# The second of sixteen feed-forward steps in plain instead of block-product form

## What is computed

```
gate  = x @ Wg.T ;  up = x @ Wu.T               # 1600 x 4096 each
gelu  = tanh(0.797885*(gate + 0.044715*gate**3)) * gate*0.5 + gate*0.5
inter = gelu * up
out   = x1 + inter @ Wd.T                        # 1600 x 512
```

## Time and profile before

| what | us |
|---|---|
| median of three runs (lowest, highest) | 2029.73 (2028.54, 2032.24) |
| the profiled execution: its time | 2030.02 |
| the profiled execution: its span, first to last instruction | 2028.2 |
| TensorE busy | 1965.3 (97%) |
| mean granted clock of TensorE | 0.990 |

### The profile page before, as it was taken

How to read it: one execution, slowest core, us unless ns; L and a number is a source line. 1 busy time by engine, 2 the same in 40 slices (tenths; PEclk the granted TensorE clock), 3 DMA queues, 4 the chain that set the end, 5 groups by cost and what they waited for, 6 DMA issues and landing times.

```text
span 2028.2 us, 34290 instructions
## 1 busy us (share of the span) xinstructions
PE 1965.3 (97%) x11480; PEld 1891.6 (93%) x11480; DVE 1603.5 (79%) x3046; ACT 1008.6 (50%) x2344; POOL 1166.8 (58%) x1323
## 2 busy tenths in 40 slices
PE   6999999999999999999999998689999999999998
PEld 5899899999999999999999998689999999999998
DVE  6777777788878788877777877878888888888875
ACT  4555455555555555555555542434444444444442
POOL 6766565533344333444333334888788888888771
PEclk9999999999999999999999999799999999999999
DMA  6434444332333323333323323211111111101101
GB/s 186 134 110 157 139 134 132 116 116 88 122 109 96 131 92 102 117 110 106 106 88 111 116 98 100 66 35 32 32 32 32 32 37 38 32 32 32 32 1 66
DMA packets 93500, 174.58 MB, mean 86 GB/s; under 512 B 13248, under 2 KB 49744, under 8 KB 91280
## 3 DMA queue, kind: packets, MB, share of 16 engines
q1 hardware_dynamic: 93328, 172.39, 26.2%
HBM read 139.00 MB, written 33.36 MB: 85 GB/s over the span
## 4 chain that ended last, share of the span: by engine, by line
PE 90%; DVE 4%; POOL 3%; ACT 1%; issue 1%; DMA 1%; SPq 0%; POOLq 0%; ACTq 0%; DVEq 0%
PE psum L377 44%; PE psum L716 21%; PE psum L410 6%; PE psum L457 3%; PE psum L442 3%; PE psum L434 3%; PE psum L463 3%; PE psum L458 3%; PE psum L507 2%; PE psum L473 1%; DVE kaT_lo L1100 0%; DMA raw<-spill_x2T 0%; DVE work L1206 0%; DMA xb<-in_x 0%; PE psum L478 0%
## 5 line engine op out<-in xcount | busy, mean ns | idle before, releaser
L1100 DVE TENSOR_TENSOR kaT_lo<-psum,kaT_hi 128x488 fp32r<-128x488 f32 (+2 forms) x384 | 216.1, 613 | 51.8 <-ACT kaT_hi L763 51.8
L823 ACT ACTIVATE work<-psum,stats,q_rstd 100x361 f32<-100x361 f32 x256 | 163.5, 650 | 185.6 <-DVE stats L1197 185.6
L377 PE MATMUL psum<-wk,ctxT_hi 128*122 128x512 f32 x768 | 242.9, 398 | 3.1 <-DVE wk L1100 3.1
L1713 POOL TENSOR_TENSOR inter_lo<-g,inter_hi 128x400 fp32r<-128x400 f32 x128 | 141.0, 1107 | 140.1 <-ACT inter_hi L763 139.2
L763 ACT CAST kaT_hi<-psum 128x488 fp32r<-128x488 f32 (+2 forms) x384 | 178.8, 540 | 74.9 <-PE psum L442 73.2
L1578 POOL TENSOR_SCALAR k_ss<-k_ss 122x4 f32<-122x4 f32 x192 | 37.1, 193 | 298.5 <-DVE k_ss L1156 297.7
L1580 POOL TENSOR_TENSOR k_ss<-k_ss,power 122x4 f32<-122x4 f32 x192 | 193.8, 1009 | 16.0
L1187 DVE TENSOR_REDUCE stats<-psum 100x2 f32<-100x722 f32 x128 | 115.8, 904 | 106.6 <-PE psum L410 106.6
L377 PE MATMUL psum<-inter_hi,down_hi 128*128 128x400 f32 x512 | 176.8, 345 | 8.2 <-ACT inter_hi L763 8.2
L377 PE MATMUL psum<-inter_lo,down_hi 128*128 128x400 f32 x512 | 176.1, 344 | 0.0
L377 PE MATMUL psum<-inter_hi,down_lo 128*128 128x400 f32 x512 | 175.9, 344 | 0.0
(11 more groups left out here) (240 smaller groups left out, 6232.6 us busy)
## 6 DMA issues: line engine op xcount, KB each, us to landing
head_w<-spill_sq SPq DMA_DIRECT2D x48, 512.0 KB, 3.5
head_w<-spill_so SPq DMA_DIRECT2D x46, 512.0 KB, 3.8
wk<-spill_sk SPq DMA_DIRECT2D x12, 1024.0 KB, 5.5
wv<-spill_sv SPq DMA_DIRECT2D x48, 256.0 KB, 2.8
spill_sq<-head_w SPq DMA_DIRECT2D x16, 512.0 KB, 3.0
spill_so<-head_w SPq DMA_DIRECT2D x16, 512.0 KB, 3.0
wk_raw<-in_ctxT SPq DMA_DIRECT2D x12, 361.0 KB, 4.0
head_raw<-in_Wq SPq DMA_DIRECT2D x16, 256.0 KB, 3.6
```

The source lines that it names most:

```text
L377: last = e.matmul(out, a_, b_, start=i == 0, stop=i == len(passes) - 1)
L823: e.activation(attn[h][:, 0:SKV], bank[3 + h][0:SQ, 0:SKV], ACT.Exp, bias=st[:, h:h + 1], scale=rq[:, i * QH + h:i * QH + h + 1], accum_ou ...
L1100: e.tensor_tensor(dst, src, high.bitcast(F32), ALU.subtract).then_inc(S[sem], 1)
L1713: e.tensor_tensor(il[:, :], gact[n % 3][:, :], ih[:, :].bitcast(F32), ALU.subtract).then_inc(S["il"], 1)
```

## The change

Step 1 becomes plain as well. Its chunks come in the order 1, 3, 0, 2, so a list `STEP_CHUNK` of eight entries replaces the chunk number; block products run from step 2 on in 28 passes instead of 30. The plain weights of step 1 are split by halves of rows from the `stage` (`base_hi`, `base_lo`), without sums. The token blocks and the weight sums, now those of step 2, are made during step 1: one token quarter within each of its chunks' work, T4 of the first quarter behind the rest. The four `raw` tiles lie in other places: two where `up_kept` 1 and 2 lie later, two where `inter4` lies later; in the first pass the copies into these wait for the last token split, and the second `down` weights no longer wait for it. SP loads the codes of step 1 ahead of two residual loads, and the codes of step 2 ahead of three of the four token loads.

```diff
-PAIRS = 2 * (JT - 1)
-PLAIN = 2 * NCHUNK
+PAIRS = 2 * (JT - 2)
+STEP_CHUNK = (0, 1, 2, 3, 1, 3, 0, 2)
+STEPS = len(STEP_CHUNK)
+PLAIN = 2 * STEPS
+BASE = 4
...
+def pair_step(p):
+    return p // 2 + 2
+def blocks(jt):
+    return BASE + 2 * NP * (jt - 1) if jt > 0 else 0
...
         with ExitStack() as first:
-            raw = [tensor(first, f"raw{i}", [P, CT]) for i in range(4)]
+            raw = [tensor(first, f"raw{i}", [P, CT]) for i in range(2)]
+        kept[1] += [tensor(f, f"up_kept{i}", [P, CT]) for i in (1, 2)]
...
+        with ExitStack() as first:
+            raw += [tensor(first, f"raw{i}", [P, CT]) for i in (2, 3)]
         inter.append(pair(f, "inter4", [P, CT]))
...
-            gate_up(NCHUNK - 1)
-            for q in range(8, 12):
-                down(q)
+            for m in range(3, STEPS):
+                gate_up(m)
+                for c in range(DC):
+                    down(4 * (m - 1) + c)
             for p in range(PAIRS):
                 for at in range(2 * NP):
                     product(p, at % 2, at // 2)
                     if p == 0 and 5 <= at < 9:
-                        down(12 + at - 5)
+                        down(4 * STEPS - 4 + at - 5)
...
+            def base_hi(z, k):
+                e.wait_ge(S["scaled"], PIECES + 2 * k + 2)
+                e.wait_ge(S[("gate", "up")[k]], 2 * NCHUNK - 1 + z)
+                hi(row_half(weight[k][0][0], z), row_half(stage[k], z), "bh")
...
                 if name == "T4":
-                    e.wait_ge(S["up"], 4 * h + 4)
+                    e.wait_ge(S["up"], 2 * NCHUNK + 2 * h + 2)
...
+                if p == 0 and k == 1 and w > 0:
+                    e.wait_ge(S["tl"], 16)
...
+            for m, tokens in ((5, (0, 1)), (6, (1, 0))):
+                square(2 * m)
+                tangent(2 * m)
+                for j in range(4):
+                    token_hi(*tokens, j)
+                inter_hi(2 * m)
+                square(2 * m + 1)
+                tangent(2 * m + 1)
+                inter_hi(2 * m + 1)
+            n = PLAIN - 2
+            square(n)
+            tangent(n)
             for j in range(4):
+                token_hi(1, 1, j)
+            inter_hi(n)
+            for i in range(3):
+                for k in range(2):
+                    block_hi(2, k, i)
...
+            decode(1, 0)
             argument(5)
+            down_add(0)
             gelu(5)
...
+            token_lo(0, 0, 3)
+            for m, k, tokens in ((5, 0, (0, 1)), (6, 1, (1, 0)), (7, 2, (1, 1))):
+                decode(2, k)
+                if m == 5:
+                    token_sums(1)
+                argument(2 * m)
+                gelu(2 * m)
+                gated(2 * m)
+                for j in range(4):
+                    token_lo(*tokens, j)
+                argument(2 * m + 1)
+                gelu(2 * m + 1)
+                gated(2 * m + 1)
+                for c in range(DC):
+                    down_add(4 * (m - 1) + c)
...
             decode_scaled(PIECES)
             decode_scaled(PIECES + 1)
-            weight_sums(1, 0)
-            inter_lo(6)
+            inter_lo(4)
+            inter_lo(5)
             decode_scaled(PIECES + 2)
             decode_scaled(PIECES + 3)
-            weight_sums(1, 1)
+            base_lo(0, 0)
+            base_lo(0, 1)
+            inter_lo(6)
+            base_lo(1, 0)
+            base_lo(1, 1)
+            inter_lo(7)
+            decode_scaled(PIECES + 4)
+            inter_lo(8)
+            decode_scaled(PIECES + 5)
+            down_lo(1, 0)
+            inter_lo(9)
+            down_lo(1, 1)
+            decode_scaled(2 * PIECES)
+            decode_scaled(2 * PIECES + 1)
+            inter_lo(10)
+            weight_sums(2, 0)
+            inter_lo(11)
+            rebuild(0)
+            token_sums(0)
+            decode_scaled(2 * PIECES + 2)
+            inter_lo(12)
+            decode_scaled(2 * PIECES + 3)
+            weight_sums(2, 1)
+            inter_lo(13)
+            rebuild(1)
+            token_sums(1)
+            decode_scaled(2 * PIECES + 4)
+            decode_scaled(2 * PIECES + 5)
+            n = PLAIN - 2
+            inter_lo(n)
+            for i in range(3):
                 for k in range(2):
-                    block_lo(1, k, i)
+                    block_lo(2, k, i)
...
+            inter_lo(n + 1)
+            for i in range(4, NP):
                 for k in range(2):
-                    block_lo(1, k, i)
+                    block_lo(2, k, i)
+            down_lo(2, 0)
+            down_lo(2, 1)
...
-            for ch in range(NCHUNK - 1):
-                load_y(ch)
+            load_y(0)
             load_codes(1)
+            load_y(1)
+            load_y(2)
...
             load_raw(0, 0)
+            load_codes(2)
             load_raw(0, 1)
             load_raw(1, 0)
-            load_codes(2)
             load_raw(1, 1)
```

More of the change, by code:

```diff
@@ L1482, in vector_program @@
             norm3_lo(3)
+            decode(1, 0)
             argument(5)
+            down_add(0)
             gelu(5)
+            down_add(1)
             gated(5)
-            for q in range(4):
-                down_add(q)
-            decode(1, 0)
-            for q in range(4, 8):
-                down_add(q)
-            decode(1, 1)
-            token_sums(0)
-            argument(6)
-            for j in range(4):
-                token_lo(0, 0, j)
-            gelu(6)
-            gated(6)
-            token_sums(1)
+            down_add(2)
+            down_add(3)
+            decode(1, 1)
+            argument(6)
+            down_add(4)
+            down_add(5)
+            gelu(6)
+            down_add(6)
+            gated(6)
+            down_add(7)
+            token_sums(0)
             argument(7)
-            for j in range(4):
-                token_lo(0, 1, j)
             gelu(7)
             gated(7)
-            for q in range(8, 12):
-                down_add(q)
+            for c in range(DC):
+                down_add(8 + c)
+            decode(1, 2)
+            for j in range(3):
+                token_lo(0, 0, j)
+            argument(8)
+            gelu(8)
+            gated(8)
+            argument(9)
+            gelu(9)
+            gated(9)
+            for c in range(DC):
+                down_add(12 + c)
+            token_lo(0, 0, 3)
[11 more added lines that the diff above has]
+                gated(2 * m + 1)
+                for c in range(DC):
+                    down_add(4 * (m - 1) + c)
             def coming_codes(p, part):
-                jt, h = p // 2 + 1, p % 2
+                jt, h = pair_step(p), p % 2
                 if jt + 1 < JT and h == 0:
@@ L1566, in vector_program @@
             for d in range(8):
-                down_add(8 + 8 * PAIRS + d)
+                down_add(4 * STEPS - 8 + 8 * PAIRS + d)
         def gpsimd_program(e):
@@ L1678, in weight_sums, with base_lo @@
                 e.tensor_tensor(s4, a12, s2, ALU.subtract).then_inc(S["sums"], 1)
+            def base_lo(z, k):
+                e.wait_ge(S["bh"], 2 * z + k + 1)
+                wh, wl = (row_half(weight[k][0][part], z) for part in range(2))
+                e.tensor_tensor(wl, row_half(stage[k], z), wh.bitcast(F32), ALU.subtract).then_inc(S["bl"], 1)
             def block_lo(jt, k, i):
                 name = PRODUCTS[i][1]
-                e.wait_ge(S["bh"], 2 * NP * (jt - 1) + 2 * i + k + 1)
+                e.wait_ge(S["bh"], blocks(jt - 1) + 2 * i + k + 1)
                 wh, wl = (weight_block(k, name, weight[k][0][part], extra[k][part]) for part in range(2))
@@ L1814, in gpsimd_program @@
                 ln_rstd(2, last + b)
-            for n in (3, 4, 5):
-                inter_lo(n)
+            inter_lo(3)
             e.wait_ge(S["out"], 4 * NQ)
```

164 lines of the change are left out of this document (79 added, 85 removed).

## The result

| what | before | after |
|---|---|---|
| median, lowest to highest (us) | 2030.99, 2028.54 to 2032.88 (4 runs) | 2015.40, 2015.15 to 2017.09 (4 runs) |
| ratio, 95% interval | | 0.9926, 0.9909 to 0.9943 |
| span of the profiled execution | 2028.2 | 2013.4 |
| mean granted clock | 0.990 | 0.993 |

The kernel is 15.6 us faster, 0.7%. (The kernel before has a fourth run here; with it its median is 1.3 us above the one given ahead.) The forecast was 2009 us, 20.8 less than the profiled execution before. The measured 2015.40 is 6 us more: within the stated range (2000 to 2020), but 1.4 above the upper end of the case that the forecast called its own (2005 to 2014).

What follows compares the result with a forecast made beforehand. TensorE, busy 97% of the span, was taken as the bound: matmuls plus holes. From 2030.02 us, 39.5 for the old opening was removed, 4.35 for four groups and 14.3 for new losses given back: 2009.2 us, range 2000 to 2020.

Steps and rivals of the forecast that it cites:

- the case that the forecast called its own: Whole kernel: holes of 10 to 19 us in all, time 2005 to 2014 us, chance 0.55.
- The old opening: Block form's passes 0 and 1 before the change: cost 39.5 us more than their matmuls, to be removed.
- the walk: Instruction-by-instruction dating of the engines' queues through step 1 and the new opening; 1.5 us added for waits and slips.
- the rival of the other side: Opening only moves behind step 1: same 39.5 us there, 2034.4 us; chance 0.06 slower, 0.02 within 0.2%.
- the loss behind step 1: New opening after step 1: TensorE loses 14.3 us to waits, slow clock and slips.
- late at the first product: First block product after step 1: TensorE waits about 6.5 us, product at 1319.0 against the ideal 1312.6.
- more by pass 1's opening: First down of pass 1: POOL's queue makes the loss 11.2 us by there; 1.5 added for pass 0's waits and slips.
- slow clock behind the last wait: Matmuls after the second hole, at pass 1's first down: 1.6 us lost to the lower clock.
- a warning of up to 2 us: Inside step 1, halves 12, 13 and 15: gelu waits priced at 0, up to 2 us each if DVE slips.
- The pin: Second token quarter's load, waiting for T4's split, dates POOL's chain: inter_hi(10) at 1285.6, first product at 1319.0.
- The rival that POOL and DVE exclude each other fully: Opening and step 1: DVE drags gelu 11 and 13 late, holes inside step 1; 2014 to 2022 us, chance 0.17.
- nearly all hidden: New opening: POOL's loss falls from 11.2 to 4 us or below, first hole nearly closes; 1997 to 2003 us, chance 0.2.

Runs made afterwards that it cites:

- e11: The changed kernel run again, unaltered: median 2015.10 us.
- e2: Changed kernel with DVE decoding step 2's up codes before the token sums, in its wait for the token load: median 2015.15 us.
- e5: Changed kernel with three of the second token quarter's four loads started before T4 is split, the fourth on its own semaphore: median 2014.96 us.
- e1: Changed kernel with POOL making step 2's four gate weight sums before inter_lo(10) instead of behind it: median 2016.94 us.
- e3: Changed kernel with both step 2's gate weight sums earlier on POOL and its up-code decode earlier on DVE: median 2017.55 us.
- e6: Changed kernel with DVE writing zeros for the last eight token lo parts instead of computing them: 2013.91 us (one run).
- e7: Changed kernel without POOL's four rebuilds of chunk 3's token parts, so some sums use other values: 2013.21 us (one run).
- e12: Changed kernel with 24 unused matmuls before the first block product and DVE decoding only 4 of 512 columns of step 3's gate and up codes: 2015.97 us (one run).
- e4: Changed kernel with 24 matmuls without use before the first block product: median 2013.78 us.
- e9: Changed kernel with 14 matmuls without use before the last eight downs: median 2014.26 us.

## Why the prediction was right or wrong

**Right in the frame.** The old opening was worth 39.5 us and went; the plain step costs 4.35 (passes of 23.9 us, 11,504 matmuls); step 1's own weights, base_lo on POOL, ended at 1251.7 to 1260.4, within a microsecond or so of the walk, and cost no wait; moved codes and loads on SP cost none that TensorE saw; POOL stood idle before inter_lo(10) until 1286.4 (forecast 1285.6) and then ran nearly without a pause; no hole came from pass 2 on. The opening didn't move with its size, the rival of the other side: product at 1321.9, not behind 1340.

**The term that was mis-sized is the loss behind step 1: 14.3 forecast, 19.2 measured.** By place:

| place | forecast | measured |
|---|---|---|
| late at the first product | 6.4 | 9.8 |
| more by pass 1's opening (POOL's lag, pass 0's waits, slips) | 4.8 + 1.5 | 7.7 |
| slow clock behind the last wait | 1.6 | 1.6 (e11: 0.1) |

(By e11's trace the sum is 17.7, since nothing is lost there behind the last wait.)

*At the first product*, counted from half 6 in both, the operand inter_hi(10) came 1.3 us later than in my walk, and POOL's 30 instructions took 35.4 us instead of 33.4, 0.8 of it a wait for inter_hi(13). Most of both is DVE and POOL holding each other, where my walk gave DVE's splits and sums their lengths at rest. The split of T4, ahead of the load, took 1.53 us beside POOL's down split instead of 0.51; the decode before half 12 took 5.2 us, and the one at 1275.91, with POOL at rest, 2.3; and three token splits took what DVE's timeline of the changed kernel shows.

```profile
1299.79 4.46 DVE L1158 TENSOR_TENSOR tT_lo<-raw,tT_hi 128x400 fp32r<-128x400 f32 x3
...
1306.35 0.57 DVE L1366 SCALAR_TENSOR_TENSOR g<-g,psum 128x400 f32<-128x400 f32 x1 [0.60 <-ACT g L964]
```

Three splits that take 1.54 us while POOL rests take 4.46; gelu 13 then runs at 1306.35 and half 15's gate, priced at 0 with a warning of up to 2 us, waits 3.0. The warning's second half held: e2 took this wait away and the product didn't move.

*The pin was misnamed.* I hung POOL's chain on the load of the second token quarter. e5 shortened DVE's wait for it by 2.1 us and gained 0.24 at the product, which is within what that mark varies by. What sets the date is the work of DVE and POOL together from about 1278 on: moving work within it made it later by 1.4 and 2.1 us (e1, e3) or changed nothing (e2, e5), and taking work out gave -2.4 and -3.15 (e6, e7).

*Behind the first product I named the wrong engine.* The forecast has POOL's queue set the first down of pass 1. POOL's lines of the changed kernel:

```profile
1332.10 2.52 POOL L1741 TENSOR_TENSOR down_lo<-wide,down_hi 128x512 fp32r<-128x512 f32 x2
1334.59 1.03 POOL L1793 TENSOR_TENSOR inter_lo<-g,inter_hi 128x400 fp32r<-128x400 f32 x1
1338.26 2.99 POOL L1729 TENSOR_TENSOR gate_stage<-value,gate_scale 128x512 f32<-128x512 f16 x2 [2.63 <-DVE value L1349]
```

and DVE's beside them:

```profile
1333.73 2.44 DVE L1338 SCALAR_TENSOR_TENSOR gate_packed<-gate_packed 128x512 int32<-128x512 int32 x1
```

POOL's own price was right: from the first block split's end, 1321.8, to inter_lo(18)'s end, 1355.65, are 33.9 us, of which 3.7 idle (2.63 and 1.07), so 30.2 of work against my 30.9. But it wasn't what TensorE waited for. It waited itself for DVE's codes, whose first instruction had been held until POOL's run ended at 1335.62 (2.44 us long, done at 1336.17). TensorE was stopped in pass 0 by DVE's combines and ahead of pass 1's third product by DVE's gelu, and reached the first down of pass 1, at 1357.42, without a wait, 1.8 us behind inter_lo(18). The 1.5 us that I had added for DVE in pass 0 is the part that was too small; e12 gives 2.5 us back by taking the codes from DVE alone.

*The clock* was rightly kept off the path before the last wait (e4), and rightly charged behind it, though it comes in one execution of the opening and not in the two others (e11, e9).

**The rival that POOL and DVE exclude each other fully** (0.17) named the measured time better than the forecast did: 2014 to 2022, with holes inside step 1; 2015 by its sum. Its sign was that DVE drags gelu 13 past its date, and that is the 3.0 us hole. The trace of e12 bears out its mechanism, an instruction held until POOL's run ended, and eleven more traces do. The rule of the Trainium skill (SBUF — State Buffer, Who interferes with whom), that one of the two blocks fully rather than slowing down, agrees with that row, though there the hold lasted through three of POOL's instructions, and with the `ysum` add with one input in SBUF that wasn't held. What that sum had by luck: it put the 6 us on POOL's price, where POOL's run up to the first product grew by 2.0 and the one behind it not at all; the rest came as DVE's lateness and at the kernel's end. And "nearly all hidden" (0.2) is out: the first product was later than forecast, not sooner.

**The end of the kernel** was in no term: 1.6 us of slow clock behind a wait that is in both kernels. So of the 6 us between 2009.2 and the profiled execution's 2015.15, 4.9 are the loss, 1.6 the end, -0.5 the start of half 6. The slow clock behind the last wait, 1.6 of the loss, and the start of half 6 change from one execution to the next, by more than the 1.4 us by which the forecast's own case was missed.

## What to carry to other kernels

Where VectorE and GpSimd both work from SBUF without a pause, walk them as one queue. Here an instruction of two SBUF inputs cost its length plus what was left of the other's run in twelve traces of thirteen, an idle stretch of one was no free room for its work, and only work taken out brought the date forward. Judge an edit near a wait by the date at which the wait ends, not by how long it is, and run the unaltered kernel again before a difference of one microsecond is read. A hole that disappears and comes back in the next wait was never on the path.

## What the runs showed of the hardware

- A DVE instruction on 128x4 took 3.20 us instead of 0.16 beside three GpSimd instructions in a row: it wasn't let in between them. At its full width it ended 0.54 to 0.56 us behind GpSimd's run in eleven traces, and in one (e9) it got in before the last of the run, which then took 1.49 us instead of 1.05. Token splits beside GpSimd's scaling and inter split took 1.49 us each instead of 0.51; two decode instructions with one input in SBUF took 1.15 and 1.17 us (TENSOR_SCALAR, 128x512) where others took 0.43.
- After the same wait of 2.96 us before the last downs the granted clock fell in ten of twelve traces and not in the other two; behind the wait of 1.92 us before pass 1's third product it fell in one trace of the changed kernel and not in e11 and e9, which are the same up to there (23.39, 21.83 and 21.84 us for the same 20 groups).
- The date of half 6 varied by 3.7 us between kernels that are equal up to there, more than most edits were worth, while the first product repeated to 0.26 us in five traces and the last wait's end to 0.14 in three.
